# Cross attention: rows of maxima turned by a matmul and moved inside SBUF, and a lead of 6 instead of 12

## The chip, the cores and the metric

The kernel runs on one core of one Trainium2 chip. The metric is the device time of one execution in microseconds. The kernel before was timed in three runs: median 4839.96 us, lowest 4836.34, highest 4844.47.

## The reference

A sequence of 1024 tokens of width 128 passes through four layers. Layer 0 is windowed attention with a gated feed-forward part. Layers 1, 2 and 3 hold cross attention of 16 heads of width 8 to the same context of 6404 vectors; layer 3 has masked self attention of 1024 by 1024 ahead of it. Of a cross attention this is computed:

```
q = (x @ Wq + bq).reshape(b, t, NUM_HEADS, HEAD_DIM)
k = (inp @ Wk + bk).reshape(b, s, NUM_HEADS, HEAD_DIM)
v = (inp @ Wv + bv).reshape(b, s, NUM_HEADS, HEAD_DIM)
attn = jnp.einsum('bthd,bshd->bhts', q, k)
attn = jax.nn.softmax(attn / jnp.sqrt(jnp.float32(HEAD_DIM)), axis=-1)
out = jnp.einsum('bhts,bshd->bthd', attn, v).reshape(b, t, DIM)
```

The softmax subtracts the maximum of each query's 6404 scores before the exponential. All is float32.

## The kernel before

The three cross attentions are three calls of `cross_attention` (L1313), with the same program for each; they take about three quarters of the span. Scores are made twice, since the maximum is wanted before the exponential and along the other axis.

**Maxima.** A head has 52 units (`HEAD_UNITS`): 13 chunks of 512 keys, the last of 260, by 4 tiles of queries. A unit is two matmuls (queries on the output partitions, one for each half of the 1024 queries, `max_unit`, L1390) into one of two PSUM buffers `mxb`, and one VectorE reduction over 2 x 512 elements (`take_max`, L1506) that frees the buffer. TensorE issues unit u when unit u-2 has been reduced. After a head's 52nd unit VectorE reduces the 13 chunk maxima to `nmax`, the negated maxima: 128 partitions (query within a tile) by 8 tiles, bf16 (`head_maximum`, L1513).

**Rows.** The exponential's scores want these maxima as one row per half in the queries' tile `qb`, where they are multiplied by a row of ones in the keys. SyncE (`max_rows`, L1358) waits for `head_max`, stores `nmax` turned into DRAM (`nm[h].rearrange("t p -> p t")`, 1024 elements of two bytes), waits for that store, and then issues two loads of 1 KB, one to each half's row. The first score of the head waits for both (`rows_loaded`, L1438).

**Exponentials and values.** A head has 101 slots (`HEAD_SLOTS`): a slot is a tile of 128 keys by 512 queries (keys on the output partitions), two slots for each of 50 key tiles and one for the last 4 keys. Slots are grouped by threes into an operation of 2 slots and one of 1 (`score_op`, L1433); ScalarE takes the exponential of an operation into a ring of 15 slots. `values` (L1442) multiplies the probabilities by the values in float32 with four matmuls per key tile, and VectorE copies a head's sum out of PSUM (`take_values`, L1520).

**Order on TensorE.** It is written out by hand. First 64 units (52 of head 0 and a lead of 12, `LEAD`), with the value projections among them. Then the 1077 score operations in turn; after each come those units of maxima that `units_through` (L1295) lets through, 52 for every 101 slots, and then value tiles. So the maxima run one head and 12 units ahead of the exponentials: the last unit of head h+1 is issued 23 to 25 slots before the first slot of that head, and the last unit of a layer after slot 1490 of 1616.

**Order on SyncE.** For head h: wait for the last score of head h-1 and issue the six key loads of head h+2 (1.2 MB, ring of 3 heads), store the values' sum of head h-1, and then `max_rows(h+1)`. All DMAs are issued there. In the prologue `max_rows(0)` is followed at once by the key loads of head 2.

Of the kernel before, what the change touches and what calls it, by code (L numbers as in the profile page):

```python
# [8 lines left out]
BF16 = mybir.dt.bfloat16  # L9
U8 = mybir.dt.uint8  # L10
ACT = mybir.ActivationFunctionType
ALU = mybir.AluOpType
AX = mybir.AxisListType

P = 128
N = 1024
C = 128
H = 16
HD = C // H
M = 6404  # L20
# [5 lines left out]
CHUNK = 512  # L26
# [8 lines left out]
QT = N // P  # L35
HALF = 512
# [5 lines left out]
HEAD_SLOTS = 2 * (NTILE - 1) + 1  # L42
HEAD_UNITS = 4 * NCHUNK
NOPS = 2 * (H * HEAD_SLOTS // 3) + (1 if H * HEAD_SLOTS % 3 else 0)
RING = 15
HOLD = 6
LEAD = 12
QBLOCK = 256
LAG = 2
BIG = 1.0e30  # L50
# [46 lines left out]
def scope_tools(k, ctx):  # L97
    nc = k.nc

    def sb(text, shape, dt=F32):  # L100
        return ctx.enter_context(nc.sbuf_tensor(k.name(text), shape, dt))

    def ps(text, shape):
        return ctx.enter_context(nc.psum_tensor(k.name(text), shape, F32))

    def sem(text):
        k.phase_sems.append(ctx.enter_context(nc.semaphore(k.name(text))))
        return k.phase_sems[-1]

    return sb, ps, sem  # L110
# [1168 lines left out]
def slots_through(op):  # L1279
    return 3 * ((op + 1) // 2) + (2 if op % 2 == 0 else 0)  # L1280


def op_of_slot(g):
    return 2 * (g // 3) + (1 if g % 3 == 2 else 0)
# [7 lines left out]
    return NTILE * (slots // HEAD_SLOTS) + (slots % HEAD_SLOTS) // 2  # L1292


def units_through(op):  # L1295
    return min(H * HEAD_UNITS, HEAD_UNITS + LEAD + -(-HEAD_UNITS * slots_through(op - op % 2) // HEAD_SLOTS))


def tiles_through():
# [10 lines left out]
    return done  # L1310


def cross_attention(k, kb, qb, vb, k_parts, nm, o_whole, wv):  # L1313

    nc = k.nc
    tiles_by = tiles_through()
    with ExitStack() as ctx:
        sb, ps, sem = scope_tools(k, ctx)
        sc = ps("scores", [P, 3, HALF])
        mxb = ps("max_scores", [P, 2, 2, CHUNK])  # L1320
        acc = ps("values_sum", [P, HALF])
        pr = sb("probs", [P, RING, HALF])
        mx = sb("chunk_max", [P, 2, NCHUNK, 2, QT // 2])
        nmax = sb("neg_max", [P, QT], BF16)
        acc_s = sb("values_sum_s", [P, 2, QBLOCK])

        v_product = sem("v_product")
# [3 lines left out]
        max_scores = sem("max_scores")  # L1331
        max_taken = sem("max_taken")
        head_max = sem("head_max")
        max_stored = sem("max_stored")
        rows_loaded = sem("rows_loaded")
        scores_ready = sem("scores_ready")
        exp_ready = sem("exp_ready")
# [6 lines left out]
        def keys(half, h, lo, hi):  # L1344
            at = (h % KRING) * M
            return kb[half, at + lo:at + hi]

        @block.sync
        def _(sp):
            def load_keys(h):  # L1350
                for half in range(2):
                    for p, run_length in enumerate(K_RUNS):
                        row = 64 * half + FIRST_ROW[p]
                        sp.dma_start(keys(slice(row, row + HD * run_length), h, 0, M),
                                     k_parts[h, 0:run_length].rearrange("p d n -> (p d) n"))\
                          .then_inc(keys_loaded[h % KRING], 16)

            def max_rows(h):  # L1358
                sp.wait_ge(head_max, h + 1)
                sp.dma_start(nm[h].rearrange("t p -> p t"), nmax[:],  # L1360
                             allow_slow_non_contiguous=True).then_inc(max_stored, 16)
                sp.wait_ge(max_stored, 16 * (h + 1))
                for half in range(2):
                    row = 64 * half + KROWS
                    sp.dma_start(qb[row:row + 1, HALF * h:HALF * (h + 1)].rearrange("o (j p) -> o j p", p=P),
                                 nm[h:h + 1, 4 * half:4 * (half + 1)]).then_inc(rows_loaded, 16)

            def store_values(h):
                sp.wait_ge(acc_taken, h + 1)
                sp.dma_start(o_whole[h], acc_s[:, h % 2, :]).then_inc(o_stored[h % 2], 16)  # L1370

            load_keys(0)
            load_keys(1)
            max_rows(0)
            for h in range(H):
                if h + 2 < H:
                    if h >= 1:
                        sp.wait_ge(scores_ready, op_of_slot(HEAD_SLOTS * h - 1) + 1)
                    load_keys(h + 2)
                if h >= 1:  # L1380
                    store_values(h - 1)
                if h + 1 < H:
                    max_rows(h + 1)
            store_values(H - 1)
            for b in range(2):
                sp.wait_ge(o_stored[b], 16 * (H // 2))

        @block.tensor
        def _(pe):
            def max_unit(u):  # L1390
                h, c, j = u // HEAD_UNITS, u % HEAD_UNITS // 4, u % 4
                w = min(CHUNK, M - CHUNK * c)
                if u % HEAD_UNITS == 0:
                    pe.wait_ge(keys_loaded[h % KRING], 16 * 2 * NPART * (h // KRING + 1))
                if u >= 2:
                    pe.wait_ge(max_taken, u - 1)
                for half in range(2):
                    rows = head_rows(half)
                    mm = pe.matmul(mxb[:, u % 2, half, 0:w], qb[rows, HALF * h + P * j:HALF * h + P * (j + 1)],  # L1399
                                   keys(rows, h, CHUNK * c, CHUNK * c + w), start=True, stop=True)  # L1400
                mm.then_inc(max_scores, 1)

            def value_projection(c):
# [54 lines left out]
            for c in range(3):  # L1458
                value_projection(c)
            for u in range(HEAD_UNITS + LEAD):  # L1460
                max_unit(u)
                if u % 4 == 3 and u // 4 + 3 < NCHUNK:
                    value_projection(u // 4 + 3)
            pe.wait_ge(v_copied, NCHUNK + 1)
            pe.wait_ge(v_ones, 1)
            for n in range(NOPS):
                score_op(n)
                for u in range(units_through(n - 1) if n else HEAD_UNITS + LEAD, units_through(n)):
                    max_unit(u)
                for i in range(tiles_by[n - 1] if n else 0, tiles_by[n]):  # L1470
                    values(i)
            for i in range(tiles_by[NOPS - 1], H * NTILE):
# [30 lines left out]

        @block.vector
        def _(dve):
            def take_max(u):  # L1506
                h, c, j = u // HEAD_UNITS, u % HEAD_UNITS // 4, u % 4
                w = min(CHUNK, M - CHUNK * c)
                dve.wait_ge(max_scores, u + 1)
                dve.tensor_reduce(mx[:, h % 2, c, :, j], mxb[:, u % 2, :, 0:w], AX.X, ALU.max)\  # L1510
                   .then_inc(max_taken, 1)

            def head_maximum(h):  # L1513
                dve.wait_ge(max_taken, HEAD_UNITS * (h + 1))
                if h >= 1:
                    dve.wait_ge(max_stored, 16 * h)
                dve.tensor_reduce(nmax[:], mx[:, h % 2].rearrange("p c g j -> p (g j) c"), AX.X, ALU.max, negate=True)\
                   .then_inc(head_max, 1)

            def take_values(h):  # L1520
                dve.wait_ge(tile_used, NTILE * (h + 1))
                if h >= 2:
                    dve.wait_ge(o_stored[h % 2], 16 * (h // 2))
                dve.tensor_copy(acc_s[:, h % 2, :], acc[:, 0:QBLOCK]).then_inc(acc_taken, 1)  # L1524

            dve.memset(acc[:], 0.0).then_inc(acc_zeroed, 1)  # L1526
            dve.wait_ge(acc_zeroed, 1)
            u = 0
            for h in range(H):
                last = next((n for n in range(NOPS) if tiles_by[n] >= NTILE * (h + 1)), NOPS - 1)  # L1530
                while u < units_through(last):
                    take_max(u)
                    u += 1
                    if u % HEAD_UNITS == 0:
                        head_maximum(u // HEAD_UNITS - 1)
                take_values(h)


# [66 lines left out]
def program(nc, d, out):  # L1605
    with ExitStack() as ctx:
        k = Core(nc, ctx)
        q_parts = nc.dram_tensor("q_parts", [H, NPART, HD, N], BF16).ap()
        k_parts = nc.dram_tensor("k_parts", [H, NPART, HD, M], BF16).ap()
        k_self = nc.dram_tensor("k_self", [H, NPART, HD, N], BF16).ap()  # L1610
        nm = nc.dram_tensor("neg_max_rows", [H, QT, P], BF16).ap()
        o_whole = nc.dram_tensor("o_whole", [H, P, QBLOCK], F32).ap()
        load_everything(k, d)
        windowed_layer(k, d)
# [1 line left out]
        sb, _, _ = scope_tools(k, ctx)  # L1616
        kb = k.key_ring
        qb = k.queries
# [3 lines left out]
        def attend(prefix, src, w, bq, bk, bv, then=lambda: None):  # L1622
            with ExitStack() as c2:
                vb = scope_tools(k, c2)[0]("values", [P, H, NTILE, WV])
                query_terms(k, src, k.w[prefix + w[0]], bq, q_parts)
                key_terms(k, k.w[prefix + w[1]], bk, kb, qb, q_parts, k_parts)
                cross_attention(k, kb, qb, vb, k_parts, nm, o_whole, k.w[prefix + w[2]])
            then()
            cross_output(k, o_whole, bv, o_t)

        v = k.v
# [9 lines left out]
        with ExitStack() as c2:  # L1641
# [23 lines left out]
            vb = s2("values", [P, H, QT, VC], BF16)  # L1665
# [23 lines left out]
        with ExitStack() as c3:  # L1689
            _, _, sem = scope_tools(k, c3)  # L1690
# [67 lines left out]
```

## Time and profile before

| | |
|---|---|
| median of 3 runs | 4839.96 us (4836.34 to 4844.47) |
| the profiled execution | 4841.48 us, span 4839.6 us, mean granted clock 0.853 |
| TensorE busy | 3934.6 us (81%) |
| VectorE busy | 3448.6 us (71%) |
| ScalarE busy | 2863.0 us (59%) |
| GpSimd busy | 258.7 us (5%) |
| DMA queue 1 | 103248 packets, 109.19 MB, 13.3% of 16 engines |

Busy times are sums over the whole program, which has stages of other kinds between the cross attentions. A matmul's duration in the timeline is its own; several of them overlap. "Idle before" in a row is the time that the engine stood still ahead of the instructions named, with the releaser that ended it; "remote" is a releaser that the profile could not name. The clock is given as a share of 2.4 GHz: 0.5 is 1.2 GHz.

### The profile page before, as it was taken

The numbers are of one execution on the slowest core, as the hardware profiler recorded it, in microseconds if no ns is written. First come the engines' busy times: TensorE is split into PE (matmuls) and PEld (weight loads), VectorE is DVE, ScalarE is ACT, GpSimd is POOL, SyncE is SP. The second block draws the span as 40 slices with busy tenths as digits, with TensorE's granted clock in tenths as the row PEclk, the third lists the DMA queues.
The fourth block names the chain that finished last, engine by engine and source line by source line (L and its number), as shares of the span: only waits on it lengthen the run. The fifth ranks groups of instructions, "written<-read, shape, count | busy, mean of one in ns | idle before, by whom it ended". The sixth has DMA issues, their size and how long they took to land. (4 is left out here: it accounts for less than half of the span.)

```text
span 4839.6 us, 83868 instructions
## 1 busy us (share of the span) xinstructions
PE 3934.6 (81%) x34310; PEld 1295.2 (27%) x34310; DVE 3448.6 (71%) x3258; ACT 2863.0 (59%) x4073; POOL 258.7 (5%) x183
## 2 busy tenths in 40 slices
PE   6897478988898855888988898479747988898885
PEld 2563222222222212222222222135422222222221
DVE  4332488888888615888888885389848888888871
ACT  1332157777777741677777777335414777777774
POOL 3000000000000010000000000234310000000000
PEclk9556579999998985899999989789957999999998
DMA  2000310111111012110111010100041111011100
GB/s 83 1 0 11 70 22 13 24 24 24 16 21 24 4 37 59 23 24 13 23 24 24 13 24 4 43 19 5 3 81 16 19 24 24 14 23 24 24 2 20
DMA packets 103596, 114.10 MB, mean 24 GB/s; under 512 B 58672, under 2 KB 93712, under 8 KB 98256
## 3 DMA queue, kind: packets, MB, share of 16 engines
q1 hardware_dynamic: 103248, 109.19, 13.3%
q8 instruction: 251, 4.11, 0.4%
q14 instruction: 97, 0.79, 0.1%
HBM read 83.56 MB, written 25.60 MB: 23 GB/s over the span
## 5 line engine op out<-in xcount | busy, mean ns | idle before, releaser
L1510 DVE TENSOR_REDUCE chunk_max<-max_scores 128x2 f32<-128x1024 f32 (+1 forms) x2496 | 2801.6, 1179 | 534.5 <-PE max_scores L1399 408.3
L1497 ACT ACTIVATE probs<-scores 128x512 f32<-128x512 f32 (+1 forms) x3231 | 2471.6, 809 | 907.8 <-PE scores L1425 751.9
L1425 PE MATMUL scores<-queries,key_ring 49*128 49x512 bf16 x4800 | 1288.4, 404 | 244.0 <-ACT probs L1497 129.5
L1452 PE MATMUL values_sum<-probs,values 128*9 128x256 f32 x19584 | 1446.6, 402 | 1.7 <-ACT probs L1497 1.7
L1399 PE MATMUL max_scores<-key_ring,queries 48*128 48x512 bf16 (+1 forms) x4992 | 979.0, 411 | 216.1 <-DVE chunk_max L1510 154.2
L1452 PEld LDWEIGHTS values_sum<-probs,values 128*9 128x9 f32 x19584 | 386.8, 91 | 893.6 <-issue 626.1
L1425 PEld LDWEIGHTS scores<-queries,key_ring 49*128 49x128 bf16 x4800 | 313.1, 95 | 1141.7 <-ACT probs L1497 877.6
L1399 PEld LDWEIGHTS max_scores<-key_ring,queries 48*128 48x128 bf16 x4992 | 249.7, 97 | 645.7 <-DVE chunk_max L1510 555.9
L1057 ACT ACTIVATE probs<-scores 128x512 f32<-128x512 f32 x256 | 138.5, 592 | 106.1 <-PE scores L1009 106.1
L1524 DVE COPY values_sum_s<-values_sum 128x256 f32<-128x256 f32 x48 | 20.1, 418 | 235.0 <-PE values_sum L1452 235.0
L1083 DVE TENSOR_REDUCE chunk_max<-max_scores 128x1024 f32 (+1 forms) x128 | 154.9, 1213 | 23.6 <-PE max_scores L965 23.4
L1478 ACT ACTIVATE values<-scores 128x512 f32<-128x512 f32 (+2 forms) x45 | 25.1, 565 | 213.8 <-PE scores L1409 199.8
L1074 POOL TENSOR_TENSOR probs_low<-probs 128x512 bf16<-128x512 f32 (+1 forms) x128 | 135.8, 1061 | 191.2 <-ACT probs L1057 191.2
L1106 DVE TENSOR_TENSOR probs_low<-probs 128x512 bf16<-128x512 f32 x128 | 142.4, 1114 | 1.2 <-ACT probs L1057 1.2
L1215 PE MATMUL k_product<-context,squares 128*128 128x512 f32 (+1 forms) x78 | 59.5, 907 | 101.5 <-DVE k_rest L1252 50.5
L1207 POOL MEMSET key_ring<- 32x9606 f32 x6 | 48.6, 8097 | 1646.5 <-POOLq L118 1646.3
L609 ACT ACTIVATE pt_tokens_s<-pt_tokens 128x512 f32<-128x512 f32 x32 | 19.1, 597 | 182.6 <-PE pt_extra L531 182.6
L963 PE MATMUL max_scores<-key_ring,queries 128*128 (+1 forms) x256 | 98.9, 386 | 32.1 <-DMA key_ring<-k_self 30.8
L1409 PE MATMUL scores<-squares,context 128*128 128x128 f32 x288 | 67.5, 414 | 43.2 <-DVE values_sum L1526 43.2
L965 PE MATMUL max_scores<-mask_query_key,ident_b 128*128 128x512 bf16 x256 | 98.7, 386 | 0.0
L1007 PE MATMUL scores<-queries,key_ring 128*128 (+1 forms) x256 | 97.1, 379 | 0.7 <-ACT queries L1045 0.7
L1009 PE MATMUL scores<-mask_key_query,ident_b 128*128 128x512 bf16 x256 | 96.8, 378 | 0.0
(176 smaller groups left out, 1944.1 us busy)
## 6 DMA issues: line engine op xcount, KB each, us to landing
key_ring<-k_parts SPq DMA_DIRECT2D x96, 300.2 KB
key_ring<-k_parts SPq DMA_DIRECT2D x96, 200.1 KB
k_parts<-k_part SPq DMA_DIRECT2D x108, 128.0 KB, 2.3
key_ring<-k_parts SPq DMA_DIRECT2D x96, 100.1 KB
o_whole<-values_sum_s SPq DMA_DIRECT2D x48, 128.0 KB, 8.0
queries<-q_parts SPq DMA_DIRECT2D x36, 128.0 KB
context<-in_ctx_t SPq DMA_DIRECT2D x1, 3202.0 KB, 17.5
q_parts<-q_part SPq DMA_DIRECT2D x12, 256.0 KB, 2.8
```

Of the source, the lines that this page charges most:

```text
L963: mm = pe.matmul(out, qb[:, bass.ds(qof + t * P, P)], kb[:, bass.ds(kof, cw)], start=True, stop=False)
L965: mm = pe.matmul(out, k.ident_b[:], mask[0][:, bass.ds(i * cw + t * nk, cw)], start=False, stop=True)
L1007: mm = pe.matmul(sc_bank[c][0:tk, :], kb[:, bass.ds(kof + j * tk, tk)], qb[:, bass.ds(qof + c * HALF, HALF)], start=True, stop=False)
L1057: act.activation(pr[0:tk, 2 * j + c, :], sc_bank[c][0:tk, :], ACT.Exp).then_inc(exp_ready, 1)
L1074: pool.tensor_tensor(pr_low[0:tk, 2 * j, 0:mine], pr[0:tk, 2 * j, 0:mine], high(2 * j, 0, mine), ALU.subtract).then_inc(low_pool, 1)
L1083: dve.tensor_reduce(mx[:, bass.ds(slot * (ni * QT) + i * QT + 2 * u, 2)], mx_bank[u % 2][:, :, 0:cw], AX.X, ALU.max).then_inc(max_taken, 1)
L1106: dve.tensor_tensor(pr_low[0:tk, half, 0:HALF], pr[0:tk, half, 0:HALF], high(half, 0, HALF), ALU.subtract).then_inc(low_dve, 1)
L1399: mm = pe.matmul(mxb[:, u % 2, half, 0:w], qb[rows, HALF * h + P * j:HALF * h + P * (j + 1)], keys(rows, h, CHUNK * c, CHUNK * c + w), sta ...
L1425: return pe.matmul(sc[:, g % 3, :], keys(rows, h, P * t, P * (t + 1)), qb[rows, q], start=True, stop=True)
L1452: mm = pe.matmul(acc[32 * b:32 * b + WV, 0:QBLOCK], vb[rows, h, t, :], pr[rows, slot, QBLOCK * (b % 2):QBLOCK * (b % 2 + 1)], start=(t == ...
L1497: act.activation(pr[:, a % RING:a % RING + b - a, :], sc[:, a % 3:a % 3 + b - a, :], ACT.Exp)\
L1510: dve.tensor_reduce(mx[:, h % 2, c, :, j], mxb[:, u % 2, :, 0:w], AX.X, ALU.max)\
```

## The change

The scatter of `nmax` through DRAM goes. In its place the sequence of units gets one more entry per head, 53 instead of 52 (`max_entry`, `turn_entry`): two units after the head's last one, TensorE multiplies `nmax` (as weights, 8 columns) by a 128 x 128 identity into the entry's `mxb` buffer, and VectorE copies the 8 x 128 result as bf16 into a new SBUF tile `nrow`. SyncE waits for that copy and issues two DMAs from `nrow` to the rows of `qb`, each from 4 partitions of 256 bytes. The last head's turning is the very last entry. The lead is 6 entries instead of 12, so TensorE starts the score operations after 58 entries (57 units and the turning of head 0) instead of 64 units; the turning of head h is issued 5, 6 or 7 slots (three to five score operations) before the head's first slot, and the last unit of a layer after slot 1502, its turning after slot 1508.

```diff
-LEAD = 12
+LEAD = 6
+TURN_AFTER = 2
+NENTRY = H * (HEAD_UNITS + 1)
...
-def units_through(op):
-    return min(H * HEAD_UNITS, HEAD_UNITS + LEAD + -(-HEAD_UNITS * slots_through(op - op % 2) // HEAD_SLOTS))
+def entries_through(op):
+    slots = slots_through(op - op % 2)
+    last = NENTRY if slots > HEAD_SLOTS * (H - 2) + HEAD_SLOTS - 9 else NENTRY - 1
+    return min(last, HEAD_UNITS + LEAD + -(-(HEAD_UNITS + 1) * slots // HEAD_SLOTS))
+
+
+def max_entry(w):
+
+    if w < HEAD_UNITS:
+        return 0, w
+    h, v = (w - HEAD_UNITS) // (HEAD_UNITS + 1) + 1, (w - HEAD_UNITS) % (HEAD_UNITS + 1)
+    if h == H or v == TURN_AFTER:
+        return h - 1, None
+    return h, (v if v < TURN_AFTER else v - 1)
+
+
+def turn_entry(h):
+    return NENTRY - 1 if h == H - 1 else HEAD_UNITS + h * (HEAD_UNITS + 1) + TURN_AFTER
...
+        nrow = sb("neg_max_rows", [QT, P], BF16)
...
             def max_rows(h):
-                sp.wait_ge(head_max, h + 1)
-                sp.dma_start(nm[h].rearrange("t p -> p t"), nmax[:],
-                             allow_slow_non_contiguous=True).then_inc(max_stored, 16)
-                sp.wait_ge(max_stored, 16 * (h + 1))
+                sp.wait_ge(max_taken, turn_entry(h) + 1)
                 for half in range(2):
                     row = 64 * half + KROWS
                     sp.dma_start(qb[row:row + 1, HALF * h:HALF * (h + 1)].rearrange("o (j p) -> o j p", p=P),
-                                 nm[h:h + 1, 4 * half:4 * (half + 1)]).then_inc(rows_loaded, 16)
+                                 nrow[4 * half:4 * (half + 1), :]).then_inc(rows_loaded, 16)
...
-            def max_unit(u):
-                h, c, j = u // HEAD_UNITS, u % HEAD_UNITS // 4, u % 4
-                w = min(CHUNK, M - CHUNK * c)
...
+            def max_step(w):
+                h, u = max_entry(w)
+                if w >= 2:
+                    pe.wait_ge(max_taken, w - 1)
+                if u is None:
+                    pe.wait_ge(head_max, h + 1)
+                    pe.matmul(mxb[0:QT, w % 2, 0, 0:P], nmax[:], k.ident_b[:], start=True, stop=True)\
+                      .then_inc(max_scores, 1)
+                    return
...
-            def take_max(u):
...
+            def take_entry(w):
+                h, u = max_entry(w)
+                dve.wait_ge(max_scores, w + 1)
+                if u is None:
+                    if h >= 1:
+                        dve.wait_ge(rows_loaded, 32 * h)
+                    dve.tensor_copy(nrow[:], mxb[0:QT, w % 2, 0, 0:P]).then_inc(max_taken, 1)
+                    return
...
+                if u == HEAD_UNITS - 1:
+                    dve.wait_ge(max_taken, w + 1)
+                    dve.tensor_reduce(nmax[:], mx[:, h % 2].rearrange("p c g j -> p (g j) c"), AX.X, ALU.max,
+                                      negate=True).then_inc(head_max, 1)
```

The two loops that issue units on TensorE and take them on VectorE run over entries in the same way, and the DRAM tensor `neg_max_rows` is gone.

## Rows read from the trace of the kernel before

**Rows 1.** The page, part 5; busy us, mean ns, idle before and releaser.

```profile
L1510 DVE TENSOR_REDUCE chunk_max<-max_scores 128x2 f32<-128x1024 f32 (+1 forms) x2496 | 2801.6, 1179 | 534.5 <-PE max_scores L1399 408.3
L1497 ACT ACTIVATE probs<-scores 128x512 f32<-128x512 f32 (+1 forms) x3231 | 2471.6, 809 | 907.8 <-PE scores L1425 751.9
```

**Rows 2.** Windows: length; busy (count) of PE, PEld, DVE, ACT, POOL; clock; DMA share; GB/s.

```profile
555.17:641.40 86.23, 54.27 (x212) 22.52 (x211) 71.63 (x65) 8.18 (x14) 0.00 (x0) 0.52 0.09 14
641.40:1660.20 1018.80, 913.54 (x9037) 244.09 (x9038) 870.52 (x796) 759.32 (x993) 0.00 (x0) 0.93 0.14 20
1660.20:1740.40 80.20, 66.57 (x661) 17.96 (x651) 1.84 (x5) 63.73 (x85) 0.00 (x0) 0.91 0.02 3
```

**Rows 3.** Windows for reductions alone: length, busy (count), clock, DMA share, GB/s.

```profile
696.44:723.41 26.97, 18.85 (x17) 0.75 0.35 51
723.41:756.30 32.89, 32.31 (x28) 1.00 0.01 2
1111.37:1136.33 24.96, 18.94 (x17) 0.93 0.39 54
```

**Rows 4.** Timeline of SyncE: start us, length us, instruction, count [idle before].

```profile
691.33 0.39 SPq L1360 DMA_DIRECT2D neg_max_rows<-neg_max  x1
704.37 0.52 SPq L1365 DMA_DIRECT2D queries<-neg_max_rows  x2
```

**Rows 5.** Waits of SyncE over the span: us in total, times, longest.

```profile
SPq L1365 <- DMA neg_max_rows<-neg_max: 591.3, 44, 15.0
```

**Rows 6.** Waits between 640 and 1660 us, same columns.

```profile
ACT probs L1497 <- remote: 33.8, 10, 5.1
...
DVE chunk_max L1510 <- remote: 32.3, 10, 5.3
...
PE scores L1425 <- DMA queries<-neg_max_rows: 23.4, 9, 6.5
```

**Rows 7.** Timeline from 700 us, all engines.

```profile
700.81 0.38 PE L1425 MATMUL scores<-queries,key_ring 49*128 49x512 bf16 x1
...
703.34 3.02 ACT L1497 ACTIVATE probs<-scores 128x1024 f32<-128x1024 f32 x4 [2.98 <-remote]
703.38 1.23 DVE L1510 TENSOR_REDUCE chunk_max<-max_scores 128x2 f32<-128x1024 f32 x1 [1.96 <-remote]
...
706.61 0.60 PE L1425 MATMUL scores<-queries,key_ring 49*128 49x512 bf16 x1
...
713.48 0.42 DVE L1524 COPY values_sum_s<-values_sum 128x256 f32<-128x256 f32 x1 [0.45 <-PE values_sum L1452]
```

**Rows 8.** Timeline around layer 1's first exponential scores.

```profile
621.50 0.34 DVE L1517 TENSOR_REDUCE neg_max<-chunk_max 128x8 bf16<-128x104 f32 x1
...
635.91 0.53 SPq L1365 DMA_DIRECT2D queries<-neg_max_rows  x2
636.48 2.36 SPq L1354 DMA_DIRECT2D key_ring<-k_parts  x6
...
640.34 0.61 PE L1425 MATMUL scores<-queries,key_ring 49*128 49x512 bf16 x2 [6.53 <-DMA queries<-neg_max_rows]
...
641.41 5.83 DVE L1510 TENSOR_REDUCE chunk_max<-max_scores 128x2 f32<-128x1024 f32 x5 [6.01 <-PE max_scores L1399]
```

**Rows 9.** Timeline at head 8's rows.

```profile
1188.59 0.53 SPq L1365 DMA_DIRECT2D queries<-neg_max_rows  x2
...
1190.58 0.46 PE L1425 MATMUL scores<-queries,key_ring 49*128 49x512 bf16 x1 [0.41 <-DMA queries<-neg_max_rows]
```

**Rows 10.** Groups by line and form, VectorE: its shortest copy out of PSUM.

```profile
L428 DVE COPY k_pairs<-product 128x128 f32<-128x128 f32 x8 | 2.2, 292 | 1.3 <-PE product L147 0.7
```

**Rows 11.** Timeline of ScalarE after layer 1's last maximum.

```profile
1675.00 1.51 ACT L1497 ACTIVATE probs<-scores 128x1024 f32<-128x1024 f32 x2 [4.16 <-remote]
...
1704.35 3.02 ACT L1497 ACTIVATE probs<-scores 128x1024 f32<-128x1024 f32 x4 [0.28 <-PE scores L1425]
...
1737.63 1.02 ACT L1497 ACTIVATE probs<-scores 128x1024 f32<-128x1024 f32 x1 [0.58 <-PE scores L1429]
```

More of the change, by code:

```diff
@@ L1310, in tiles_through, with cross_attention @@
     return done
-def cross_attention(k, kb, qb, vb, k_parts, nm, o_whole, wv):
+def cross_attention(k, kb, qb, vb, k_parts, o_whole, wv):
     nc = k.nc
@@ L1333, in cross_attention @@
         head_max = sem("head_max")
-        max_stored = sem("max_stored")
         rows_loaded = sem("rows_loaded")
@@ L1389, in _ @@
         def _(pe):
-            def max_unit(u):
-                h, c, j = u // HEAD_UNITS, u % HEAD_UNITS // 4, u % 4
-                w = min(CHUNK, M - CHUNK * c)
-                if u % HEAD_UNITS == 0:
+            def max_step(w):
[7 more added lines that the diff above has]
+                    return
+                c, j = u // 4, u % 4
+                width = min(CHUNK, M - CHUNK * c)
+                if u == 0:
                     pe.wait_ge(keys_loaded[h % KRING], 16 * 2 * NPART * (h // KRING + 1))
-                if u >= 2:
-                    pe.wait_ge(max_taken, u - 1)
                 for half in range(2):
                     rows = head_rows(half)
-                    mm = pe.matmul(mxb[:, u % 2, half, 0:w], qb[rows, HALF * h + P * j:HALF * h + P * (j + 1)],
-                                   keys(rows, h, CHUNK * c, CHUNK * c + w), start=True, stop=True)
+                    mm = pe.matmul(mxb[:, w % 2, half, 0:width], qb[rows, HALF * h + P * j:HALF * h + P * (j + 1)],
+                                   keys(rows, h, CHUNK * c, CHUNK * c + width), start=True, stop=True)
                 mm.then_inc(max_scores, 1)
@@ L1460, in _ @@
             for u in range(HEAD_UNITS + LEAD):
-                max_unit(u)
+                max_step(u)
                 if u % 4 == 3 and u // 4 + 3 < NCHUNK:
@@ L1467, in _ @@
                 score_op(n)
-                for u in range(units_through(n - 1) if n else HEAD_UNITS + LEAD, units_through(n)):
-                    max_unit(u)
+                for w in range(entries_through(n - 1) if n else HEAD_UNITS + LEAD, entries_through(n)):
+                    max_step(w)
                 for i in range(tiles_by[n - 1] if n else 0, tiles_by[n]):
@@ L1505, in _ @@
         def _(dve):
-            def take_max(u):
[L1507 to L1510, printed above, removed]
-                   .then_inc(max_taken, 1)
[L1513 to L1518, printed above, removed]
+            def take_entry(w):
[6 more added lines that the diff above has]
+                    return
+                c, j = u // 4, u % 4
+                width = min(CHUNK, M - CHUNK * c)
+                dve.tensor_reduce(mx[:, h % 2, c, :, j], mxb[:, w % 2, :, 0:width], AX.X, ALU.max)\
+                   .then_inc(max_taken, 1)
+                if u == HEAD_UNITS - 1:
+                    dve.wait_ge(max_taken, w + 1)
+                    dve.tensor_reduce(nmax[:], mx[:, h % 2].rearrange("p c g j -> p (g j) c"), AX.X, ALU.max,
+                                      negate=True).then_inc(head_max, 1)
             def take_values(h):
@@ L1527, in _ @@
             dve.wait_ge(acc_zeroed, 1)
-            u = 0
+            w = 0
             for h in range(H):
                 last = next((n for n in range(NOPS) if tiles_by[n] >= NTILE * (h + 1)), NOPS - 1)
[L1531 to L1535, printed above, removed]
+                while w < entries_through(last):
+                    take_entry(w)
+                    w += 1
                 take_values(h)
@@ L1610, in program @@
         k_self = nc.dram_tensor("k_self", [H, NPART, HD, N], BF16).ap()
-        nm = nc.dram_tensor("neg_max_rows", [H, QT, P], BF16).ap()
         o_whole = nc.dram_tensor("o_whole", [H, P, QBLOCK], F32).ap()
@@ L1626, in attend @@
                 key_terms(k, k.w[prefix + w[1]], bk, kb, qb, q_parts, k_parts)
-                cross_attention(k, kb, qb, vb, k_parts, nm, o_whole, k.w[prefix + w[2]])
+                cross_attention(k, kb, qb, vb, k_parts, o_whole, k.w[prefix + w[2]])
             then()
```

## The prediction

> **What bounds the kernel now.** I read the page's groups by line first, then the windows of one cross attention, then the timeline. In the groups, the reader is to see that VectorE's reductions of the maxima are the largest work, 2496 of them with 2801.6 us, ahead of ScalarE's exponentials with 2471.6 us [rows 1]. All of both lie in the three cross attentions. The windows cut the first of them into a start of 86.2 us (maxima alone), a body of 1018.8 us (maxima beside exponentials) and an end of 80.2 us (exponentials alone) [rows 2]; the other two layers repeat this.
>
> In the body the windows over the reductions show two paces [rows 3]. A quiet stretch of 28 units takes 32.89 us, 1.175 us a unit, with the clock at 1.00 and VectorE busy for 32.31 us of it: there VectorE is the bound. The 16 units around the rows' transfer take 26.97 or 24.96 us (the 17th record only touches the edge) where 16 x 1.175 = 18.8 would do. Every head has both stretches. The sum over the body: 768 units x 1.175 = 902.4 us, and 14 copies of the values at 0.45 idle + 0.42 [rows 7] = 12.2 us, make 914.6 us. Measured are 1018.8, so 104.2 us are disturbance, 7.4 us for each of 14 heads.
>
> What disturbs is seen in three places. SyncE issues the scatter at 691.33 and can issue the loads of the rows only at 704.37 [rows 4]; over the span it waited 44 times for the scatter, 13.4 us on average [rows 5]. Within that time, at 701 to 703 us, ScalarE and VectorE both stand still and begin again together at 703.34 and 703.38, "remote" [rows 7]; the body holds ten such waits of each, 33.8 and 32.3 us, and nine waits of TensorE for the rows themselves, 23.4 us [rows 6]. Then the same matmul takes 0.60 us instead of 0.38 [rows 7]: after the pause TensorE is at the lower of its two levels, 1.2 GHz, and these windows have mean clocks of 0.75 and 0.93 [rows 3].
>
> **The scatter goes.** I count all of the 7.4 us per head as its doing: the joint pauses, the waits for the rows and the slow clock behind them. The bounds are zero (the pauses have another cause) and 7.4; I take 7.4, since the quiet stretches with the same work and no scatter in flight show no trace of it, and put what comes in its place in the next terms.
>
> A rule of the Trainium skill speaks against this. The page "SBUF — State Buffer", section "Who interferes with whom", says that a DMA never contends with a compute engine. By that rule the joint pauses in [rows 6] would not be the scatter's and would stay; what that gives is the third rival below.
>
> **The turning entry.** Per head one matmul, one copy and two DMAs are added. The copy's nearest row is VectorE's shortest copy out of PSUM, 0.29 us [rows 10]. The entry also takes one of the two PSUM buffers, and TensorE can issue the unit after it only when the unit before it has been reduced, so behind a short entry VectorE waits for a matmul. Below, the entry costs its 0.29; above, a whole unit's place, 1.18. I take 0.9, nearer the upper end, because the entries are also let through by slots, at the pace of whole units. The matmul itself lies on TensorE while VectorE is at work; if TensorE were the bound it would cost about one of the 0.38 us matmuls.
>
> **The rows' wait, with the lead of 6.** Let T be the moment when TensorE issues the turning. VectorE still has one unit to reduce, 1.18, then the copy, 0.29: T+1.5. SyncE then issues both moves. The time from issue to the first score that waits is 1.99 us at head 8 [rows 9] and 4.43 us where six key loads are issued right behind the rows [rows 8]. A move inside SBUF of 4 x 256 bytes is not in the trace; I take the 1.99, as in the body the key loads now wait for the last score of the head and so come after the moves, and keep 4.43 as the other end. So the rows are there at T+3.5, at worst T+5.9. TensorE comes to the head's first slot 5 to 7 slots after the turning; ScalarE in its quiet pace takes 3.30 us for 6 slots, 0.55 each [rows 11], so it comes at T+2.8 to T+3.8. TensorE waits 0 to 0.7 us, and VectorE has one or two units in hand, 1.2 to 2.4 us. I take 0.5 us of idle VectorE per head, between 0 and 2.5. Queued behind the waiting score on TensorE are the next units of maxima and the value tiles; behind SyncE's wait are only the key loads two heads ahead and the store of a sum, which have a head's time, some 60 us.
>
> **The start.** The negated maxima of head 0 are ready at 621.84; the first score starts at 640.34 and VectorE's next unit at 641.41, after 6.01 us idle [rows 8]. Now two units of 1.14 follow, the copy of 0.29, and the moves with key loads behind them, 4.43: first score at 628.8, next unit 1.07 later, at 629.9. The units let through before need VectorE until 627.8 anyway. So the body begins 11.5 us earlier.
>
> **The body.** 832 - 57 = 775 units are left: 775 x 1.175 = 910.6. With 14 copies, 12.2, 14 turnings at 0.9, 12.6, and 14 waits at 0.5, 7.0, it takes 942.4 us instead of 1018.8, 76.4 less.
>
> **The end.** Behind the last unit stood 126 slots, now 114. At 0.55 us a slot, and 2.8 us from the last exponential at 1737.63 to the end [rows 11], the old end would be 72.1 us without disturbance; it is 80.2, with a pause of 4.16 us at 1675.00 [rows 11]. The new one: 62.7 + 2.8 + 0.5 = 66.0 us, 14.2 less.
>
> **The sum.** 11.5 + 76.4 + 14.2 = 102.1 us per cross attention, 306 for three. The profiled execution took 4841.5 us, so 4535; the median of the runs lies 1.5 us below that execution, which gives 4534. The rest of the program isn't touched. The bounds of the single terms: turning at 0.29 and no wait for rows, and a start that VectorE alone sets, 4534 - 26 - 23 - 6 = 4479; turning at 1.18 and 2.5 us of wait, 4534 + 12 + 90 = 4636.
>
> **Rivals.**
>
> *The rows come late at every head.* The move needs the 4.43 us: rows at T+5.9, TensorE waits some 2.6 us, longer than what VectorE has in hand, and the clock falls after it as it does now. Then about 4 us per head are lost instead of 0.5, 45 x 3.5 = 158: 4690. For it: three to five operations are a short lead, and the issue of six key loads falls near the moves. Against it: 1.99 us were measured where the key loads came later. The Trainium skill, "DMA: Bandwidth & Descriptors", section "Specifications", says that below 512 bytes the DMA reads, modifies and writes; that would favour this rival, as the new pieces have 256 bytes, and no row here shows it.
>
> *The pauses stay.* The remote waits are not the scatter's. They keep 32.3 / 14 = 2.3 us per head and their share of the rest: of 7.4, 2.3 are remote and about 1.2 waits for rows, so 2.3/3.5 of the other 3.9, 2.6. 45 x 4.9 = 220: 4755. Against it: the pauses lie in the scatter's 13 us and none in the quiet stretches.
>
> *Slower.* The place is the move from four partitions to one. If it took as long as the scatter, 13.4 us and a little more for its landing, the rows would come at T+15.5 with TensorE there at T+3.3; VectorE, with 1.8 us in hand, would idle 10.4 us, and some 2 us would go to the clock: 11.9 more than forecast, at 48 heads 571, so 5105. It decides from an idle VectorE of 0.5 + 306/48 = 6.9 us per head, a move of about 10 us. Against it: the 1 KB loads into the same rows take 2 us, and the scatter's cost goes with its 1024 elements.
>
> *Nothing changes.* Only if the quiet stretches' pace were lost by the new order; I see no row for it.
>
> **Chances.** Forecast 0.71, late rows 0.17, pauses stay 0.07, slower 0.03, no change 0.02. A measurement of this kernel tells 0.2% from no change, 10 us. The first three are faster: 0.95; same 0.02; slower 0.03. The predicted time is the first case's. The range is 4480 to 4680: the forecast's own bounds, and upward the nearer half of the late rows.
>
> **What would show it.** No "remote" waits in the bodies and no pause of all engines; windows over any head's 16 units at the row transfer near 20 us with the clock at 1.00; a body of about 942 us, a start of 75 and an end of 66; waits of TensorE for the rows below 1 us a head. Late rows would show as 2 to 4 us of TensorE waiting for the DMA, and clock 0.5 behind it. I am wrong if the quiet pace is no longer 1.175 us a unit, or if pauses remain with no scatter in flight.

## The result

| | median us | runs | ratio to the kernel before, 95% |
|---|---|---|---|
| kernel before | 4838.15 | 4 (4828.01 to 4844.47) | |
| changed kernel | 4599.1 | 4 (4596.61 to 4605.47) | 0.951 (0.949 to 0.9529) |

The change saves 239 us, where 304 were forecast, and lies in the range. The page of the changed kernel has these two groups in the place of [rows 1] (busy us, mean ns, idle before and releaser):

```profile
L1537 DVE TENSOR_REDUCE chunk_max<-max_scores 128x2 f32<-128x1024 f32 (+1 forms) x2496 | 2801.3, 1179 | 325.4 <-PE max_scores L1420 304.6
L1518 ACT ACTIVATE probs<-scores 128x512 f32<-128x512 f32 (+1 forms) x3231 | 2475.9, 809 | 664.0 <-PE scores L1446 634.3
```

The same number of reductions at the same 1179 ns; VectorE's idle time before them went from 534.5 to 325.4 us, and "remote" is no longer among its releasers.

The windows of layer 1 answer to [rows 2]; columns are length, busy time (count) of PE, PEld, DVE, ACT and POOL, clock, DMA share, GB/s. The body now begins with the 58th entry's reduction and has 775 units instead of 768.

```profile
554.35:627.66 73.31, 50.26 (x197) 21.97 (x195) 63.87 (x59) 8.42 (x14) 0.00 (x0) 0.52 0.09 14
627.66:1594.28 966.62, 895.88 (x9125) 244.37 (x9129) 880.62 (x817) 766.95 (x1001) 0.00 (x0) 0.96 0.14 21
1594.28:1660.24 65.96, 57.40 (x604) 16.31 (x592) 1.75 (x6) 57.73 (x77) 0.00 (x0) 0.97 0.01 3
```

Start 73.3 us, body 966.6, end 66.0: forecast were 74.7, 942.4 and 66.0. The other two bodies take 964.4 and 964.5 us (from their first to their last reduction). So start and end came as forecast, and the whole miss of 65 us lies in the bodies, 22 to 24 us in each.

The waits inside the first body answer to [rows 6]. Remote waits of ScalarE and VectorE, 33.8 and 32.3 us before, are gone, and so are the waits of TensorE for the rows, 23.4 us; what VectorE still waits for is TensorE:

```profile
ACT probs L1518 <- PE scores L1446: 185.4, 428, 1.8
...
DVE chunk_max L1537 <- PE max_scores L1420: 74.7, 129, 1.8
```

SyncE's timeline answers to [rows 4]: the two moves stand alone, 2.9 us ahead of the next key loads.

```profile
687.92 1.20 SPq L1380 DMA_DIRECT2D queries<-neg_max_rows  x2
690.85 2.16 SPq L1372 DMA_DIRECT2D key_ring<-k_parts  x6
```

The turning's own cost, in the group of its copy (duration in ns, least, median, most; first and last start in us):

```profile
L1533 DVE CAST neg_max_rows<-max_scores x48: 268/269/279, 623.5 to 4477.0; 8x128 bf16<-8x128 f32 x48
```

Where the bodies lost their time is seen in windows cut by the units of a head (unit 0 is its first; "units 4 to 12" runs from the start of unit 4 to the start of unit 12). The boundary, where the exponentials pass from one head to the next, comes while the maxima, a head ahead, are at units 3 to 6. The windows are, of the changed kernel, units 4 to 12, 12 to 20 and 20 to 48 of head 7, and units 4 to 12 of head 8. The first of them holds the copy of the values' sum, so it should take 8 x 1.175 + 0.87 = 10.3 us.

```profile
1017.39:1030.35 12.96, 11.86 (x103) 2.85 (x95) 9.67 (x10) 7.77 (x11) 0.00 (x0) 0.74 0.67 106
1030.35:1039.71 9.36, 8.89 (x96) 2.26 (x89) 9.22 (x9) 7.70 (x11) 0.00 (x0) 1.00 0.01 3
1039.71:1072.97 33.26, 31.14 (x328) 8.51 (x326) 32.40 (x29) 27.54 (x37) 0.00 (x0) 1.00 0.00 1
1083.12:1092.85 9.73, 8.79 (x88) 2.12 (x87) 9.55 (x10) 7.57 (x11) 0.00 (x0) 1.00 0.85 119
```

Head 7 takes 12.96 us with a mean clock of 0.74, head 8 takes 9.73 us at 1.00. The rest of the head is nearly as it was in the quiet stretch of [rows 3]: 33.26 us for 28 units, where that took 32.89. Counted over the start times of all reductions, heads 2 to 15 of three layers (42), the units 4 to 12 take 11.65 us on average, 1.4 more than they should, and in 34 of the 42 the clock is at 1.2 GHz for a stretch of 3.4 or 6.8 us that begins in the 8th, 9th or 10th unit. Before such a stretch TensorE's timeline shows this (start us, length us, engine, line, operation, count):

```profile
692.99 1.16 PE L1473 MATMUL values_sum<-probs,values 128*9 128x256 f32 x16
694.09 0.39 PE L1446 MATMUL scores<-queries,key_ring 49*128 49x512 bf16 x2
694.32 0.38 PE L1420 MATMUL max_scores<-key_ring,queries 48*128 48x512 bf16 x2
695.00 0.39 PE L1420 MATMUL max_scores<-key_ring,queries 48*128 48x512 bf16 x2 [0.30 <-DVE chunk_max L1537]
695.23 0.76 PE L1446 MATMUL scores<-queries,key_ring 49*128 49x512 bf16 x3
696.46 0.39 PE L1420 MATMUL max_scores<-key_ring,queries 48*128 48x512 bf16 x2 [0.47 <-DVE chunk_max L1537]
696.69 0.38 PE L1446 MATMUL scores<-queries,key_ring 49*128 49x512 bf16 x1
697.00 1.66 PE L1473 MATMUL values_sum<-probs,values 128*9 128x256 f32 x16
698.59 0.61 PE L1446 MATMUL scores<-queries,key_ring 49*128 49x512 bf16 x2
```

From 694.1 to 697.0 us there are two groups of scores and no value matmul (L1473), with TensorE idle for 0.30 and 0.47 us between the units; at 698.59 a score matmul takes 0.61 us where it took 0.39. In each of the 34 heads the fall begins behind the last value matmul ahead of such a hole and at most 0.3 us behind the hole's end. The kernel makes this hole itself: `tiles_through` holds the value tiles of a new head back until 6 slots of it are issued (`HOLD`), since the one PSUM buffer of the sum has to be copied first. One group of three slots at each boundary has no tiles, and the four or five groups behind it have two each, where one and two take turns otherwise. This is in both kernels.

### The profile page after: what moved, and what is told of

Its sections match the earlier page's. It is cut to its first block and busy times, and to the rows that moved or that the text cites. A ratio compares the mean times of both kernels' runs of the same rounds, so it can differ in the third digit from the quotient of the medians.

```text
span 4603.5 us, 83947 instructions
## 1 busy us (share of the span) xinstructions
PE 3836.9 (83%) x34296; PEld 1292.0 (28%) x34358; DVE 3455.6 (75%) x3306; ACT 2867.1 (62%) x4073; POOL 258.4 (6%) x183
## 3 DMA queue, kind: packets, MB, share of 16 engines
q1 hardware_dynamic: 53904, 109.09, 13.4%
## 5 line engine op out<-in xcount | busy, mean ns | idle before, releaser
L1537 DVE TENSOR_REDUCE chunk_max<-max_scores 128x2 f32<-128x1024 f32 (+1 forms) x2496 | 2801.3, 1179 | 325.4 <-PE max_scores L1420 304.6
L1473 PE MATMUL values_sum<-probs,values 128*9 128x256 f32 x19584 | 1402.7, 392 | 1.7 <-ACT probs L1518 1.7
L1446 PE MATMUL scores<-queries,key_ring 49*128 49x512 bf16 x4800 | 1251.4, 392 | 80.7 <-ACT probs L1518 48.9
L1420 PE MATMUL max_scores<-key_ring,queries 48*128 48x512 bf16 (+1 forms) x4992 | 949.7, 396 | 246.5 <-DVE chunk_max L1537 195.0
L1473 PEld LDWEIGHTS values_sum<-probs,values 128*9 128x9 f32 x19584 | 383.8, 90 | 852.9 <-issue 575.3
L1085 DVE TENSOR_REDUCE chunk_max<-max_scores 128x1024 f32 (+1 forms) x128 | 154.9, 1213 | 21.4 <-PE max_scores L967 21.3
```

The lines of the kernel that those rows point to most:

```text
L1085: dve.tensor_reduce(mx[:, bass.ds(slot * (ni * QT) + i * QT + 2 * u, 2)], mx_bank[u % 2][:, :, 0:cw], AX.X, ALU.max).then_inc(max_taken, 1)
L1420: mm = pe.matmul(mxb[:, w % 2, half, 0:width], qb[rows, HALF * h + P * j:HALF * h + P * (j + 1)], keys(rows, h, CHUNK * c, CHUNK * c + wid ...
L1446: return pe.matmul(sc[:, g % 3, :], keys(rows, h, P * t, P * (t + 1)), qb[rows, q], start=True, stop=True)
L1473: mm = pe.matmul(acc[32 * b:32 * b + WV, 0:QBLOCK], vb[rows, h, t, :], pr[rows, slot, QBLOCK * (b % 2):QBLOCK * (b % 2 + 1)], start=(t == ...
L1537: dve.tensor_reduce(mx[:, h % 2, c, :, j], mxb[:, w % 2, :, 0:width], AX.X, ALU.max)\
```

## The experiments

Each was timed with the kernel before on the same chip; ratios have their 95% interval.

| kernel | median us | ratio to before |
|---|---|---|
| turning, lead 12 | 4600.3 | 0.9505 (0.948 to 0.9529) |
| scatter, lead 6 | 5172.5 | 1.0692 (1.067 to 1.0714) |
| changed + idle scatter | 4737.0 | 0.9779 (0.9752 to 0.9806) |
| changed + idle block store | 4591.7 | 0.9498 (0.9471 to 0.9525) |
| changed, hold 3 | 4540.2 | 0.9362 (0.9327 to 0.9398) |
| changed, hold 12 | 4680.1 | 0.9652 (0.9616 to 0.9688) |
| changed, keys later | 4599.9 | 0.9488 (0.9451 to 0.9525) |
| changed, lead 5 | 4616.5 | 0.952 (0.9483 to 0.9557) |
| changed, hold 3, lead 12 | 4549.7 | 0.9279 (0.9242 to 0.9316) |
| changed, hold 3, lead 9 | 4511.7 | 0.9193 (0.9155 to 0.9232) |
| changed, hold 0 | 4579.6 | 0.9341 (0.9304 to 0.9377) |
| before, hold 3 | 4868.5 | 0.9931 (0.9908 to 0.9954) |

The first four ran with the kernel before at 4838.3 us, the next four at 4846.6, the last four, on another chip, at 4898.0. Across the two chips the medians are compared, not the ratios, and the traces bear this out for kernels without a scatter: the changed kernel with a hold of 0 (second chip) and with a hold of 3 (first chip) take 10.56 and 10.56 us for the eight units around a head's first, and 42.65 and 42.69 us for units 12 to 48, on average.

### Is it the scatter? A scatter that nobody waits for, and a block of the same bytes

```diff
+            def idle_store(h):
+                sp.wait_ge(scores_ready, op_of_slot(HEAD_SLOTS * h + 40) + 1)
+                sp.dma_start(nm[h].rearrange("t p -> p t"), nmax[:],
+                             allow_slow_non_contiguous=True).then_inc(max_stored, 16)
...
                 if h + 1 < H:
+                    idle_store(h)
                     max_rows(h + 1)
```

The second kernel has `nm` as [H, P, QT] and stores to `nm[h]`, untransposed (128 pieces of 16 bytes). In both VectorE waits for the last store before it overwrites `nmax`, a head later.

> The changed kernel with the old scatter to DRAM put back for the first 15 heads of each layer, at slot 40 of the head, where nothing waits for it until the next head's maxima. Theory (the scatter itself makes the joint pauses and the clock falls behind them): a pause of 2 to 5 us some 9 to 13 us behind each scatter, in what was a quiet stretch, and 2 to 5 us per head: 4599 + 45 x 2.3 to 4.9 = 4700 to 4820 us. Rival (pauses come from elsewhere, DMA and engines don't contend): 4599 us and no pauses.

> The same extra store at the same place, but untransposed: 128 pieces of 16 bytes instead of 1024 of 2. Theory (what hurts is the number of two-byte elements): within 0.3% of the changed kernel, 4599 us, no pauses. Rival (any store of the negated maxima in this place hurts): like the scatter.

The scatter costs 137.9 us (4737.0 against 4599.1), 3.1 us per scatter; the block of the same 2 KB costs nothing that can be told (4591.7). The timeline of the scatter's kernel, 12 us behind its issue, in what is a quiet stretch in the changed kernel:

```profile
649.60 0.40 SPq L1386 DMA_DIRECT2D neg_max_rows<-neg_max  x1
...
658.96 0.38 PE L1428 MATMUL max_scores<-key_ring,queries 48*128 48x512 bf16 x2
661.61 3.49 DVE L1545 TENSOR_REDUCE chunk_max<-max_scores 128x2 f32<-128x1024 f32 x3 [3.33 <-remote]
661.64 1.51 ACT L1526 ACTIVATE probs<-scores 128x512 f32<-128x512 f32 x2 [2.97 <-remote]
...
662.89 0.61 PE L1428 MATMUL max_scores<-key_ring,queries 48*128 48x512 bf16 x2 [3.55 <-DVE chunk_max L1545]
```

TensorE still works at 658.96 us, when VectorE already stands still; nobody waits for the store, and yet VectorE and ScalarE begin again together, 12 us after the scatter was issued. TensorE waits for VectorE, and its next matmul is then at the low clock. Over the span VectorE has these waits, against none in the changed kernel:

```profile
DVE chunk_max L1545 <- remote: 88.3, 28, 5.5
```

These 28 waits end 10.3 to 14.4 us after a scatter's issue. The loss is where the scatter is: units 20 to 48 take 36.66 us on average instead of 33.13, and 33.13 with the block store. So the scatter itself makes the joint pauses and the clock falls behind them, and what does it is that the 2 KB go in 1024 pieces of two bytes; with 128 pieces of 16 it does not happen. The number and the size of the pieces were not varied apart. The theory's span of 2.3 to 4.9 us per head held, at its lower end.

### Turning and lead apart

```diff
-LEAD = 6
+LEAD = 12
```

> The changed kernel with the lead put back to 12: the turning alone. Theory (the scatter was the disturbance, the lead only moves work from start and end into the body): start 6 units or 6.9 us longer, end 12 slots or 6.6 us longer, body 6 units or 7 us shorter, so about 6.5 us per layer more than the changed kernel, 4618 us. The clock drop at unit 8 to 10 of each head: if the head's boundary makes it, it moves with the boundary, to unit 14 to 16; if the turning makes it, it stays 8 units behind the turning. Rival (the lead of 6 is too short and costs the missing 1.6 us per head): the body loses that, 45 x 1.6 = 72 us, and it ends at 4545 us.

The median is 4600.3 us, that of the changed kernel within its noise: the whole gain is the turning's, and the lead of 6 gave nothing on top. The 18 us less that 4600 is than 4618 are in no single place. In the profiled executions the three starts are 17.5 us longer in all (20.7 expected) and the three ends 12.4 (19.8 expected). In equal units the bodies are 11 us shorter, nearly all of it in layer 1; in the other two layers they are equal within 2 us. The rival's 72 us did not come. The clock fall moved with the boundary: in 22 heads it begins in the 14th unit and in 4 later, where it began in the 8th to 10th in the changed kernel, 26 falls against 34. Head 12, units 4 to 12 and 12 to 20, in the lead-12 kernel:

```profile
1327.48:1337.29 9.81, 8.84 (x96) 2.48 (x93) 9.22 (x8) 8.13 (x11) 0.00 (x0) 1.00 0.26 46
1337.29:1349.76 12.47, 11.53 (x92) 2.86 (x96) 9.66 (x10) 7.56 (x11) 0.00 (x0) 0.73 0.55 75
```

In the changed kernel the same head's two windows take 12.87 and 9.58 us.

```diff
-LEAD = 12
+LEAD = 6
```
in the kernel before:

> The kernel before with its scatter, the lead alone cut to 6. Theory: the last unit of a head is issued 12 slots, about 7 us, ahead of the first score that needs its rows, and the scatter with the loads takes 16 us, so TensorE waits some 9 us per head instead of 1 to 2, VectorE idles 6 to 7 us more, and the saved start and end (20 us) don't pay for it: about 5100 us. Rival (the lead is where the gain comes from): not slower than before, 4838 us or less.

5172.5 us, 7% slower than before and 72 more than expected: the lead of 6 can't be had with the scatter. TensorE's waits for the rows in layer 1's body:

```profile
PE scores L1425 <- DMA queries<-neg_max_rows: 162.2, 15, 14.6
```

That is 10.8 us each, where nine waits of 2.6 us stood in [rows 6].

### What holds the body up: the hole in the value tiles, or the key loads?

```diff
-HOLD = 6
+HOLD = 3
```
and 12 in the second kernel; in the third, the key loads' wait becomes `op_of_slot(HEAD_SLOTS * h + 39) + 1`.

> The changed kernel with the value tiles of a new head held back for 3 slots instead of 6. Theory (at each boundary one group of three slots has no value matmul, TensorE stands still a moment, its clock falls to 1.2 GHz for 3 to 7 us and the units behind the boundary become TensorE's): with the hole closed the clock stays at 1.00, the eight units behind the boundary take 10.1 us at every head instead of 9.7 to 13.0, 45 x 1.5 = 70 us less: 4530 us. Rival (the six key loads that start at the boundary take the time): no change, 4599 us.

> The same with 12 slots. Theory (the hole): three groups without value matmuls, the clock falls at every head and for longer, 1 to 3 us more per head: 4650 to 4740 us. Rival (key loads): 4599 us.

> The changed kernel with the key loads of head h+2 issued after slot 39 of head h instead of at its first slot. Theory (the hole): the clock still falls behind the boundary, 4599 us within 0.3%. Rival (the key loads cost at the boundary): the clock fall goes or moves to slot 39 and beyond; if it goes, 4530 us.

With 3 the time falls to 4540.2 us, 59 less; with 12 it rises to 4680.1, 81 more, with a fall of the clock in all of the 42 heads; later key loads leave it at 4599.9, with falls in 36. First the hold of 3: TensorE's timeline at the same boundary, and the window over head 7's units 4 to 12.

```profile
696.47 0.39 PE L1446 MATMUL scores<-queries,key_ring 49*128 49x512 bf16 x2
696.69 0.38 PE L1420 MATMUL max_scores<-key_ring,queries 48*128 48x512 bf16 x2
697.38 0.39 PE L1420 MATMUL max_scores<-key_ring,queries 48*128 48x512 bf16 x2 [0.30 <-DVE chunk_max L1537]
697.60 0.38 PE L1446 MATMUL scores<-queries,key_ring 49*128 49x512 bf16 x1
697.91 1.05 PE L1473 MATMUL values_sum<-probs,values 128*9 128x256 f32 x16
698.90 0.39 PE L1446 MATMUL scores<-queries,key_ring 49*128 49x512 bf16 x2
```

```profile
1012.80:1022.62 9.82, 8.97 (x99) 2.28 (x95) 9.57 (x10) 7.67 (x11) 0.00 (x0) 1.00 0.87 121
```

A pair of value tiles follows at 697.91, the clock stays up, 9.82 us instead of 12.96. With the hold of 12 both windows of head 7 (units 4 to 12, 12 to 20) have low clocks:

```profile
1029.09:1038.96 9.87, 8.18 (x59) 1.55 (x55) 9.57 (x10) 7.53 (x11) 0.00 (x0) 0.79 0.87 122
1038.96:1050.86 11.90, 11.39 (x127) 3.35 (x119) 9.40 (x9) 7.93 (x11) 0.00 (x0) 0.89 0.10 16
```

With later key loads, units 4 to 12 and 20 to 48 of head 7:

```profile
1017.65:1030.62 12.97, 11.87 (x103) 2.86 (x95) 9.66 (x10) 7.78 (x11) 0.00 (x0) 0.74 0.00 1
1039.98:1073.23 33.25, 31.14 (x328) 8.50 (x326) 32.39 (x29) 27.54 (x37) 0.00 (x0) 1.00 0.29 42
```

The DMA share is 0.00 instead of 0.67 at the boundary and 0.29 instead of 0.00 in the quiet stretch, and the times are those of the changed kernel to 0.01 us. The key loads don't matter; the hole does. With the hold of 3 the units 4 to 12 take 10.39 us on average, against 11.65: 1.26 us, times 45 heads 57 of the 59 us saved. The clock still falls in 11 of the 42 heads there, and the trace shows what these have in common. A head has 101 slots, which is not a multiple of three, so its first slot stands at another place in its group for each of three heads in turn. At every third boundary the first value tile comes so early that TensorE has to wait 0.78 us for VectorE's copy of the old sum, and all 11 falls are at these 15 boundaries. The row of that wait, over the span:

```profile
PE values_sum L1473 <- DVE values_sum_s L1548: 13.6, 26, 0.8
```

```diff
-HOLD = 6
+HOLD = 0
```

> The changed kernel with no hold: the first value tile of a new head comes one group of slots earlier and TensorE waits for VectorE's copy of the old sum. Theory (what costs is TensorE standing still at the boundary): a wait of about 0.5 to 1 us in TensorE per head in place of the hole, between the holds of 3 and 6: 4540 to 4580 us. Rival (the less hold the better): below 4540 us.

4579.6 us, between the two, as expected; units 4 to 12 take 11.30 us on average, between 10.39 and 11.65. In the order of issue this hold differs from that of 3 only at every third boundary, and there TensorE now waits 1.53 us for the copy instead of 0.78; the clock falls in the 8th unit in 17 heads, 12 of them at these boundaries.

```profile
PE values_sum L1473 <- DVE values_sum_s L1548: 25.7, 27, 1.5
```

The hold of 3 in the kernel before, by the same line:

> The kernel before, scatter and lead of 12, with the hold of 3. Theory (of the 7.4 us per head that I gave to the scatter, some 1.5 are the hole in the value tiles and were there before): 4840 - 45 x 1.3 = 4780 us, if the clock is not low there already behind the scatter's pause; where it is, less is saved, 4810. Rival (the hole matters only in the changed kernel): 4840 us.

Ratio 0.9931, 29 us less than before on that chip (4898.0), about 0.65 us per head: the hole cost in the kernel before too, about half of what it costs now; that the other half lay behind the scatter's own pauses and slow clock is what I take it for, not shown.

### How tight is the lead, and the best version

```diff
-LEAD = 6
+LEAD = 5
```

> The changed kernel with a lead of 5: the turning is issued 3 to 5 slots ahead of the head's first slot instead of 5 to 7. Theory (at 6 the rows are just in time, with the wait of TensorE near zero): the rows are 1.1 us later against the first slot, TensorE waits about 1 us per head for them, and up to 0.5 us of it reaches VectorE, 0 to 25 us in all, with 2 us saved at start and end of each layer: 4593 to 4620 us. Rival (the move takes much less than I count): no wait at all, 4593 us.

4616.5 us, inside what was expected. The rows are now waited for, where the changed kernel had 0.5 us of it in all:

```profile
PE scores L1446 <- DMA queries<-neg_max_rows: 13.0, 20, 1.7
```

```diff
-LEAD = 6
+LEAD = 12
...
-HOLD = 6
+HOLD = 3
```

> Turning, hold of 3 and the lead of 12. Theory (with 12 the turning and the boundary lie 10 units apart, and TensorE has slack at each; the clock falls at the boundary in 11 of 42 heads with the lead of 6): start 6.9 and end 4 us longer per layer as in the lead-12 run, body about 10 us shorter in equal units, so even at about 4540 us; lower, down to 4520, if the last clock falls go too. Rival (the lead of 6 is itself worth the 20 us of start and end): 4570 us.

The same with a lead of 9:

> Turning, hold of 3 and a lead of 9. By the theory between the leads of 6 and 12, 4525 to 4545 us, the lowest of the three if the distance of 5 units between turning and boundary is enough to keep the clock; by the rival 4555 us.

With a hold of 3 throughout: 4549.7 us with a lead of 12 and 4511.7 with 9, both on the second chip, and 4540.2 with 6, on the first. The lead of 12 came out between theory and rival, and that of 9 is lower than I expected. Windows of head 7, the eight units around its first one and units 4 to 12, lead 9:

```profile
997.32:1006.92 9.60, 9.24 (x105) 2.75 (x105) 7.96 (x11) 8.80 (x12) 0.00 (x0) 1.00 0.01 2
1006.92:1016.77 9.85, 9.16 (x104) 2.34 (x96) 9.64 (x10) 7.69 (x11) 0.00 (x0) 1.00 0.61 92
```

and the first of these with hold 3 and lead 6:

```profile
1002.28:1012.80 10.52, 10.00 (x120) 2.89 (x108) 8.05 (x11) 9.06 (x13) 0.00 (x0) 1.00 0.00 0
```

9.60 against 10.52 us. On average over 42 heads it is 9.58 against 10.56, and times 42 these are 41 us; start and end, longer by 5 us per layer, take a part of it back. That the head's last four, narrow units and the turning fit better between the groups of scores with 9 is my reading, which no run tests. The clock falls in 6 of the 42 heads with 9, in 11 with 6 and in 9 with 12. This kernel (the turning, a hold of 3, a lead of 9) is 8.1% below the one before and the best that ran.

## Why the prediction was right, and what it missed

**The scatter goes: right in kind, too large.** Joint pauses, waits for rows and the clock behind them went away, and the idle scatter brought the pauses back where nothing waits. But I took the whole 7.4 us per head as the scatter's. A head takes 69.4 us on average before and 64.9 now, with 1.2 us of turning in it, so 5.7 of the 7.4 went. The idle scatter shows 3.1 of these; the waits for the rows in [rows 6] are 1.7 per head at most; the rest no run assigns. What stayed is mostly the hole in the value tiles: closing it saves 1.3 us per head in the changed kernel and 0.65 in the one before, and it stood there unseen, in the same 16 units as the scatter. The quiet stretches could not show it, since they hold no boundary; I took their pace for the whole head. That is the step that failed, the argument that stretches without a scatter show no trace of the disturbance.

**The pauses are the scatter's.** They are in the traces and come back with a store that nobody waits for, so here the measurement decides against the rule of the Trainium skill that I weighed ("SBUF — State Buffer", "Who interferes with whom"), at least for what the engines see: VectorE and ScalarE stood still, and TensorE with them as it waits for VectorE. What stopped them may be the semaphores on their way and not their data; no run here tells these two apart. (The rival that goes by this rule, *The pauses stay*, is the second in my list and not the third.) Another is borne out: the Trainium skill, "DMA: Bandwidth & Descriptors", section "Rules for kernel authors", says that a last dimension that is not contiguous becomes one descriptor per element, and asks for a contiguous one. The trace agrees: queue 1 has 103248 packets before and 53904 after, and 49152 of the packets before, 48 x 1024, have two bytes. The block store of the same bytes cost nothing, the scatter 3.1 us.

**The turning entry, 0.9 us.** The eight units around a head's first (its first four and the four ahead of them) took 9.38 us before and 10.56 now: 1.18, a whole unit's place, my upper bound; 0.28 x 42 = 12 us of the 65. The copy alone takes 0.27 us. With a lead of 9 it costs 0.2.

**The rows' wait, 0.5 us.** I took 0.5 us per head; TensorE waits for the rows 0.5 us in the whole program, and pieces of 256 bytes did not make the move late. At the start, with six key loads right behind it, it took 2.6 us to the first score, where I had taken 4.43 from [rows 8]:

```profile
623.76 1.42 SPq L1380 DMA_DIRECT2D queries<-neg_max_rows  x2
...
625.22 2.31 SPq L1372 DMA_DIRECT2D key_ring<-k_parts  x6
...
626.34 0.61 PE L1446 MATMUL scores<-queries,key_ring 49*128 49x512 bf16 x2 [0.19 <-DMA queries<-neg_max_rows]
```

So the rival of late rows is out at a lead of 6, and begins at 5 (waits of 1.7 us at most).

**Start, end.** 11.5 us and 14.2 us forecast; 12.9 (86.2 against 73.3) and 14.2 measured. But the run with a lead of 12 says that this was no gain of the lead: what it saves there the body gives back.

**The sum of the miss**, per head: boundary +1.4, turning +0.3, units 12 to 48 +0.4 (42.7 us on average against 36 x 1.175 = 42.3), rows' wait -0.5: 1.6 us, times 42 heads, 67 us, of the 68 that the three bodies take more than forecast; the start gives 4 of it back.

**The signs.** Of those that I named, the pauses' end, the start, the end and the rows' wait came true. The body of 942 us and the clock of 1.00 at the boundary did not: the 16 units there take 21.3 us instead of 20, and the clock falls in 34 of 42 heads. That the changed kernel with a hold of 3 comes to 4540 us, near the 4534 forecast, is in part luck: the rows' wait that I took too high makes up for the turning that I took too low.

## What to carry to other kernels

Price a disturbance by a stretch that has the same work and lacks only the cause; a boundary that coincides with it has to be priced apart, and one run that moves the suspect elsewhere tells the two apart. A transposed store of two-byte elements is not free because nobody waits for it: here it paid to turn the tile on TensorE and to move whole rows. Where TensorE is not the bound, see that its work has no hole at stage boundaries, since the clock that it loses makes it the bound for several microseconds.

## What I had not expected

A 2 KB store in 1024 elements makes VectorE and ScalarE stand still, and TensorE wait for them, mostly for 2 to 5 us, until 10 to 14 us after its issue, without any data or wait in common; not every scatter does so (28 remote waits of VectorE in 45 scatters). The kernel before took 4838 to 4847 us in three groups of runs and 4898 on the chip of the last; VectorE's remote waits in the hold-3 run there were 134.1 us, against 105.8 in the trace of before. No one kernel without a scatter ran on both chips, but stretches without one are equal there (see behind the table of the experiments). The difference stands behind the scatter: units 4 to 20 take 27.7 us there with a hold of 3 and 27.1 in the trace of before, and with the 0.65 us that the hold saves this is 1.2 us per head, 56 us in all, of the 58. Why the scatter costs more on that chip stays open. And a fall of the clock stood behind one group without value matmuls in 34 of 42 heads, with idle times of only 0.30 and 0.47 us in the one shown.
